# Up weights of the experts loaded in the last group of heads, down weights split in seven groups, five of eight rests by PE

## What is computed

```python
q  = ln(fp8_linear(ln_out, wq));  k = ln(fp8_linear(ln_out, wk));  v = fp8_linear(ln_out, wv)
core = softmax(q k^T) v                      # 16 heads in 8 groups
xout = softmax(ln(fp8_linear(ln_out, wqx)) ln(cond wkx)^T) (cond wvx)
x = layernorm(x + fp8(concat(core, xout)) wproj)

weights = softmax(softcap(x w_gate)) * top2_mask          # 8 experts, 2 of them per row
for e in range(8):
    out += (silu(x w1[e]) * (x w3[e])) w2[e] * weights[:, e]
x = layernorm(x + out)
```

## Time and profile before

| | us |
|---|---|
| median of 3 runs | 1407.73 (1407.22 to 1408.06) |
| the profiled execution | 1406.92 |
| its span, first to last instruction | 1405.2 |

### The profile page before, as it was taken

One profiled execution on the slowest core, in us unless ns is written; L12 is line 12 of the kernel. 1 busy time (PEld: TensorE's weight loads), 2 busy tenths in 40 slices (PEclk: granted clock), 3 DMA queues, 4 the chain that ended last, 5 costly groups with the idle time before them and its releaser, 6 DMA issues. The chain is left out here.

```text
span 1405.2 us, 28389 instructions
## 1 busy us (share of the span) xinstructions
PE 1317.8 (94%) x8483; PEld 1096.3 (78%) x8483; DVE 1044.0 (74%) x2583; ACT 940.9 (67%) x3183; POOL 917.5 (65%) x1109
## 2 busy tenths in 40 slices
PE   9999988896799999999999999999999978999992
PEld 4445666663599999999998998999898855899891
DVE  5899768897788888888887777777778847444443
ACT  3997457775588888888887777777777746323321
POOL 4996237774278787787887766766767844455542
PEclk9999999998999999999999999999999999999996
DMA  9421110000102002012020020020100248677764
GB/s 343 158 117 64 36 46 2 1 2 1 60 1 91 1 1 92 1 39 73 24 97 14 1 91 1 16 76 2 46 1 24 76 157 322 149 162 164 164 159 135
DMA packets 55160, 105.85 MB, mean 75 GB/s; under 512 B 5052, under 2 KB 33668, under 8 KB 52708
## 3 DMA queue, kind: packets, MB, share of 16 engines
q1 hardware_dynamic: 46100, 84.90, 17.7%
q0 software_dynamic: 7488, 10.23, 4.6%
q10 hardware_dynamic: 1424, 8.91, 1.6%
HBM read 75.58 MB, written 28.44 MB: 74 GB/s over the span
## 5 line engine op out<-in xcount | busy, mean ns | idle before, releaser
L1921 ACT ACTIVATE pr_<-ps,neg_ 128x128 f32<-128x128 f32 x512 | 181.1, 367 | 61.4 <-DVE neg_ L2091 61.4
L1938 ACT ACTIVATE y<-ps,invsm 128x128 bf16<-128x128 f32 x512 | 145.9, 368 | 62.3 <-PE ps L1826 62.0
L1999 POOL TENSOR_TENSOR rstd<-var,half 128x6 f32<-128x6 f32 x128 | 172.5, 1348 | 10.0
L2010 POOL TENSOR_TENSOR z<-t,m 128x512 fp32r<-128x512 bf16 x128 | 148.7, 1161 | 3.4 <-DVE t L2117 3.4
L1808 PEld LDWEIGHTS ps<-qkt 128*128 128x128 f32 x1024 | 134.0, 191 | 10.4 <-ACT qkt L1905 2.8
L1994 POOL TENSOR_TENSOR var<-stat,deps 128x6 f32<-128x6 f32 x128 | 26.1, 204 | 175.1 <-DVE stat L2071 175.0
L1837 PE MATMUL ps<-phi,z 128*128 128x256 f32 x512 | 138.1, 303 | 1.0 <-POOL z L2010 1.0
L1808 PE MATMUL ps<-qkt 128*128 128x128 f32 x1024 | 135.3, 275 | 2.5 <-ACT qkt L1913 2.3
L1826 PE MATMUL ps<-spare 128*128 128x256 f32 x512 | 131.9, 379 | 2.8 <-ACT spare L1929 2.8
L2003 POOL TENSOR_TENSOR pr_<-pr_,rec_ 128x512 f32<-128x512 f32 x128 | 132.7, 1037 | 1.8 <-DVE rec_ L2098 1.8
L1837 PE MATMUL ps<-plo,z 128*128 128x256 f32 x512 | 127.7, 280 | 0.0
(11 more groups left out here) (367 smaller groups left out, 4046.3 us busy)
## 6 DMA issues: line engine op xcount, KB each, us to landing
f_w_low<-w_low SPq DMA_DIRECT2D x39, 512.0 KB
centred<-raw_weights ACTq DMA_DIRECT2D x8, 1024.0 KB, 3.9
w_low<-w_dram SPq DMA_DIRECT2D x8, 1024.0 KB, 10.7
aw_st<-centred SPq DMA_DIRECT2D x7, 1024.0 KB, 6.3
raw_weights<-wself_dram SPq DMA_DIRECT2D x4, 1024.0 KB, 13.7
raw_weights<-wcross_dram SPq DMA_DIRECT2D x4, 1024.0 KB, 14.4
w_rest<-w_dram SPq DMA_DIRECT2D x8, 512.0 KB, 3.9
w_high<-w_top SPq DMA_DIRECT2D x8, 512.0 KB, 3.0
```

The costliest lines, as they stand in the source:

```text
L1921: ins = act.activation(pr[:, u.par, h, :], bS[:, h * S:(h + 1) * S], ACT.Exp, bias=neg[:, u.par, h:h + 1], accum_out=tot[:, u.par, h:h + 1])
L1938: ins = act.activation(y[:, u.par, h * S:(h + 1) * S], bO[:, h * S:(h + 1) * S], ACT.Copy, scale=invsm[:, head:head + 1])
L1999: pool.tensor_tensor(rstd[:, u.par, 0:6], v, half[:, :], ALU.pow).then_inc(s_rstd, 1)
L2010: pool.tensor_tensor(z[:, u.par, :], t[:, u.par, :], m[:, u.par, :], ALU.subtract).then_inc(s_z, 1)
```

## The change

- The tile of up weights (`w_low`, 64 KB per partition) is placed at the right end of memory, over tiles of the attention stage that are dead in its last group: slot 0 of `whi`, `wlo`, `phi`, `plo`, the codes of the values (now a tile of its own, `xval`), the raw weights, the raw context and both tiles of the down-weight split. The turned rows and the codes for the cross queries move to the left end.
- SP issues all eight loads of up weights at place 6 of the last group, after five waits (`load_up`).
- The split of the down weights is therefore done within the first seven groups: sixteen halves at places 3 and 13 of these and at place 8 of groups 1 and 4; SP stores a finished expert and loads the next one in the same step.
- The gate layer loads the high parts of the down weights; ACT rounds pieces 0 and 2 in it.
- PE makes the rests of five pieces instead of four (0, 2, 3, 5, 7), of which 2, 3 and 5 stand ahead of the map; only 7 stands behind it. VectorE is left with 1, 4 and 6. ACT's order is 3, 5, 1, 7, 4, 6, with the copies between (`HIGH_ORDER`).

```diff
-WARM_UNITS, WARM_PRODUCTS, WARM_AT_END, BY_PE = 4, (3, 4), 15, (0, 2, 3, 7)
+WARM_UNITS, WARM_PRODUCTS, WARM_AT_END, BY_PE = 4, (3, 4), 15, (0, 2, 3, 5, 7)
+HIGH_ORDER = (0, 2, 3, 5, 1, 7, 4, 6)
...
+        with ExitStack() as home:
+            up = sbuf(home, "w_low", [P, 2, E, 2 * I], F32R, side="right")
...
+        w2_units = sorted([B * w + b for w in range(2 * PAIRS - 1) for b in (3, 13)] + [B + 8, PAIRS * B + 8])
+
         def w2_half(u):
 
-            return slice(0, I) if u.b == 3 else slice(I, 2 * I) if u.b == 13 else None
+            if u.n not in w2_units:
+                return None
+            e, half = divmod(w2_units.index(u.n), 2)
+            return e, half, slice(half * I, (half + 1) * I)
...
+                def store_w2(u):
+                    if w2_half(u) is None:
                         return
...
+                    e, half, part = w2_half(u)
+                    if half:
+                        sp.wait_ge(s_w2_low, 2 * e + 2)
+                        for name, a in (("w2_high", w2_high), ("w2_low", w2_low)):
+                            sp.dma_start(io[name][e, :, :], a[:, :].bitcast(F32)).then_inc(w2_stored, 16)
+                        if e + 1 < E:
+                            load_w2(e + 1)
+
+                def load_up(u):
+                    if not u.last or u.b != UP_AT:
                         return
...
+                    sp.wait_ge(s_w, u.w * B)
+                    sp.wait_ge(weights.s_lo, weights.count(u.w, PIECES - 1))
+                    sp.wait_ge(weights.s_plo, weights.count(u.w, 1, 2))
+                    sp.wait_ge(s_clo, B)
+                    sp.wait_ge(w2_stored, 16 * 2 * E)
+                    for q in range(UP_PIECES):
+                        i, e = up_place(q)
+                        sp.dma_start(up[:, i, e, :].bitcast(F32).rearrange("p e (k n) -> p e k n", k=CB),
+                                     io[("w1", "w3")[i]][e].rearrange("e (k p) n -> p e k n", p=P)).then_inc(up_loaded[q], 16)
...
-                in_steps([(load_w2, 0), (load_weights, 0), (load_context, 0), (store_w2, 0), (store_rows, 7)])
+                in_steps([(first_w2, 0), (load_weights, 0), (load_context, 0), (store_w2, 0), (load_up, 0), (store_rows, 7)])
...
@@ gate_layer
-                experts.load_up(sp, io, range(0, UP_PIECES // 2))
                 for name in ("rows_x", "sums"):
                     sp.dma_start(io[name][(B - 1) * S:B * S, :], X[:, B - 1, :]).then_inc(experts.stored, 16)
+                experts.load_w2(sp, io)
...
                 experts.split_high(act, 0)
+                experts.split_high(act, 2)
...
@@ moe_layer, SP
-                experts.load_up(sp, io, range(UP_PIECES // 2, UP_PIECES))
-                experts.load_w2(sp, io)
...
@@ moe_layer, PE
                 subtract(2)
+                subtract(3)
+                subtract(5)
                 for c in range(2 * B // CHUNK):
...
-                subtract(3)
                 subtract(7)
...
@@ moe_layer, ACT
-                experts.split_high(act, 1)
                 keep(0)
-                experts.split_high(act, 2)
                 experts.split_high(act, 3)
                 keep(2)
-                for q in range(4, UP_PIECES):
+                experts.split_high(act, 5)
+                keep(3)
+                experts.split_high(act, 1)
+                keep(5)
+                for q in (7, 4, 6):
                     experts.split_high(act, q)
-                keep(3)
                 keep(7)
...
@@ moe_layer, VectorE
                 experts.split_low(dve, 4)
-                experts.split_low(dve, 5)
                 experts.split_low(dve, 6)
```

More of the change, by code:

```diff
@@ L185, in build @@
                     w2_stored = nc.alloc_semaphore(name="w2_stored")
-                    layer(quant_layer, columns_ctx, rows_ctx, row_stats, quant, rows_stored, w2_stored)
+                    up_loaded = [nc.alloc_semaphore(name=f"experts_up_loaded{q}") for q in range(UP_PIECES)]
+                    layer(quant_layer, xcross, up, up_loaded, row_stats, quant, rows_stored, w2_stored)
         args.pop("XT")
         if stop > 5:
-            experts = Experts(ctx, sbuf, nc, rows_stored, w2_stored)
+            experts = Experts(ctx, sbuf, nc, up, up_loaded, rows_stored, w2_stored)
             layer(gate_layer, experts)
@@ L1384, with __init__ @@
 class Weights:
-    def __init__(self, tag, quant, first, io, sem, sbuf, ctx):
+    def __init__(self, tag, quant, first, io, sem, sbuf, ctx, side="left"):
         self.quant, self.first, self.io = quant, first, io
-        self.st = sbuf(ctx, tag + "st", [P, PIECES, UW], F32)
-        self.rows = sbuf(ctx, tag + "rows", [P, 2, 2, C], F32)
+        self.st = sbuf(ctx, tag + "st", [P, PIECES, UW], F32, side=side)
+        self.rows = sbuf(ctx, tag + "rows", [P, 2, 2, C], F32, side=side)
         self.d_w, self.d_p, self.s_hi, self.s_lo, self.s_phi, self.s_plo = (
@@ L1611, in in_steps, with attention @@
                 stage(Pair(step - lag))
-def attention(xq, xcross, row_stats, quant, rows_stored, w2_stored, nc, io, sem, sbuf, X, XT, small, ident, ps, col, cols):
+def attention(xq, xval, xcross, up, up_loaded, row_stats, quant, rows_stored, w2_stored, nc, io, sem, sbuf, X, XT, small, ident, ps, col, cols):
     ctx = ExitStack()
@@ L1861, in _ @@
                 for _ in range(WARM_AT_END):
-                    pe.matmul(bQ[:, :], columns(CROSS, 0)[:, 0, :], whi[:, 1, 0, 0, :], start=True, stop=True)
+                    pe.matmul(bQ[:, :], columns(CROSS, 0)[:, 0, :], whi[1][:, 0, 0, :], start=True, stop=True)
             @block.scalar
@@ L1894, in prepare @@
                         weights.rows_high(act, u.w + 1, i)
-                    part = w2_half(u)
-                    if part is not None:
-                        act.wait_ge(d_w2, 16 * u.w + 16)
+                    if w2_half(u) is not None:
+                        e, half, part = w2_half(u)
+                        act.wait_ge(d_w2, 16 * e + 16)
                         act.activation(w2_high[:, part], w2_low[:, part].bitcast(F32), ACT.Copy).then_inc(s_w2_high, 1)
@@ L1983, in prepare @@
                         weights.rows_low(pool, u.w + 1, i)
-                    part = w2_half(u)
-                    if part is not None:
-                        pool.wait_ge(s_w2_high, 2 * u.w + 1 + (part.start > 0))
+                    if w2_half(u) is not None:
+                        e, half, part = w2_half(u)
+                        pool.wait_ge(s_w2_high, 2 * e + half + 1)
                         pool.tensor_tensor(w2_low[:, part], w2_low[:, part].bitcast(F32), w2_high[:, part].bitcast(F32),
@@ L2139, in _, with up_place, __init__ @@
                 dve.wait_ge(s_last_normed, 1)
+UP_AT = 6
+def up_place(q):
+    e, i = divmod(q, 2)
+    return i, slice(e * PIECE, (e + 1) * PIECE)
 class Experts:
-    def __init__(self, ctx, sbuf, nc, stored, w2_stored):
+    def __init__(self, ctx, sbuf, nc, up, up_loaded, stored, w2_stored):
         self.gate = sbuf(ctx, "moe_gate", [P, CB, ROWS], F32)
-        self.low = sbuf(ctx, "w_low", [P, 2, E, 2 * I], F32R)
         self.high = sbuf(ctx, "w_high", [P, 2, E, 2 * I], F32R)
         self.w2 = sbuf(ctx, "w2", [P, E, 2 * I], F32R)
-        self.up_loaded = [nc.alloc_semaphore(name=f"experts_up_loaded{q}") for q in range(UP_PIECES)]
+        sbuf(ctx, "w_low_home", [P, 2, E, 2 * I], F32R, side="right")
+        self.low, self.up_loaded = up, up_loaded
         self.w2_loaded, self.s_hi, self.s_lo = (
@@ L2349, in chunks @@
         def chunks(q):
-            i, e = experts.place(q)
+            i, e = up_place(q)
             first = BY_PE.index(q) * PIECE * CB
@@ L2385, in subtract @@
                 def subtract(q):
-                    pe.wait_ge(experts.s_hi, q + 1)
+                    experts.made_high(pe, q)
                     for at, (i, e, c) in chunks(q):
```

106 lines of the change are left out of this document (50 added, 56 removed).

## The result

| | before, us | after, us |
|---|---|---|
| median of 18 runs each | 1413.43 (1407.22 to 1416.61) | 1415.88 (1414.60 to 1419.66) |
| the profiled execution | 1406.92 | 1415.52 |
| its span | 1405.2 | 1413.8 |

The account below looks back on a forecast made before the run. The kernel's end was taken to stand where the expert loop's chain of 39 scatter-adds starts; a later map less time saved behind it moved the first up product by +3.1 us, so 1407.73 + 3.1 = 1410.8 us, range 1406.5 to 1413.2.

Parts of the forecast that it names:

- The gathers, taken as hidden: Behind the token list: the second gather of x lands at 1190.5, 2.7 us after issue, hidden under VectorE's splits.
- the terms of VectorE (1.49, 4.40, 0.80): From list to first up product: 1.49 us to the next splits, 4.40 for two splits, 0.80 from rest of x.
- Rival 1: Behind the list: the second gather trails VectorE's last split, first up product at 1193.2, +4.7 us, 1412.4 us; chance 0.18.
- saves 2.2 us behind the list: Piece 5 taken off VectorE saves 2.2 us behind the list and costs 4.4 us ahead of it.
- Part 1: Last group of heads: eight 1 MB loads of up weights, about 1051 to 1073 us, are covered and cost 0.
- rival 4: Attention stage: the 8 MB of loads slow it by 0.5 us or more, giving 1411.3 to 1413 us; chance 0.07.
- its own sign: Train of adds: the prediction is wrong if the train's own step, 4.8 us, changes; only its start should move.
- Part 2: Attention stage: the sixteen down-weight halves, done within seven groups, cost 0 in sum.
- Part 3: Gate layer: with weights in place, ACT's rounding ends sooner and the next layer starts 0.83 us earlier.
- Part 4: Ahead of the map: twelve chunks instead of four, map at 1177.45, 7.7 us new wait; first up product +3.1 us.
- Rival 2: Ahead of the map: PE's clock does not fall, map at 1175.7, first product +1.4 us, 1409.1 us; chance 0.33.
- Rival 3: Ahead of the map: chunks run faster without transfers, at 0.65 us each -3.9 us, 1403.8 us; chance 0.10, other gains included.

Follow-up runs that it names:

- lower group: The kernel before, unchanged, in its faster executions: five of its 18 runs, from 1407.2 to 1408.1 us.
- upper group: The kernel before, unchanged, in its slower executions: thirteen of its 18 runs, from 1413.1 to 1416.6 us; the profiled one took 1413.27 us.

## Why the prediction was right and wrong

The forecast was +3.1 us on 1407.73, that is 1410.8 us and +0.22%, in a range of 1406.5 to 1413.2. The time of the changed kernel, 1415.88 us, lies outside. Set against what the forecast stood on, an execution of the lower group, the change cost 8.2 us in the medians and 8.6 in the profiles. The ratio, +0.28%, is near the forecast by luck, as the paragraph on the level shows. Counted in steps of the two profiles:

| step | forecast | measured |
|---|---|---|
| start of the gate layer | 0 | +1.31 |
| to piece 0 | -0.83 | -0.83 |
| to the map | +7.73 | +5.95 |
| to the list | 0 | -0.08 |
| to the first up product | -3.76 | -0.92 |
| to the first add | 0 | +1.67 |
| first to last add | 0 | +1.3 |
| sum | +3.1 | +8.4 |

**The gathers, taken as hidden.** This is the step that failed. The sum had the second gather in under the splits, at the 2.7 us of the quickest row. It took 6.54 from its issue to PE's use, and from the list to the first up product it took 9.53 us, where the sum had 6.69: 2.8 us too few. With the rests of the down weights held back it was 6.59, so the terms of VectorE (1.49, 4.40, 0.80) were right and the gather was the missing one. That run's median, 1412.21, lies inside the range: it was this wait and the cold first tile behind it, 4.5 us together, that took the time out of the range.

Rival 1 named the gather, but for the wrong reason and from a misread row: it had it trail VectorE's splits by 2.1 us, 8.2 behind the list. In the row of PE's weight load the wait is put down to the gather; PE's own row of the same products, shown above, names VectorE's rest of x, as it does in every profile of the kernel before. The gather was beside the same three loads there, and at the 6.54 us measured after it would have been in at 1187.4 (an estimate), ahead of 1188.31. So the 10.45 us behind the list covered it, and the change shortened what covered it. For the same reason the prediction's "saves 2.2 us behind the list" is too little: its own sum gains 3.76 there, 1.56 of it because PE's piece 3 no longer stands behind the map.

The Trainium skill (SBUF — State Buffer, "SBUF: two separate sides") has a transfer issued by GpSimd seem blocked while VectorE holds the shared port pair. It says so for VectorE's two-port modes; for an instruction with two SBUF operands, like the splits, it names only a conflict with GpSimd instructions that read SBUF. The run with the rests held back shows that the 3 us were not such a block: the gather came that much sooner under the same splits. What the splits do go with is a longer issue on POOL, 1.7 to 1.9 us, against 0.95 behind them. In another place the trace agrees with that section, which has one engine wait for a whole instruction of the other: the router's instructions of 0.17 us took 1.2 beside POOL's of 1.27.

**Behind the first product.** The prediction moved the loop as a block. But PE's 3.48 us of waiting for the gather put the clock to 0.57 at 1194 to 1198, and the first tile took 1.67 us more. Without that wait it took 10.3 again.

**Part 1, the loads at no cost.** Right in the attention stage: first to last residual 745.9 us after, 746.5 before, the loads issued at 1052.18 and the next row store at 1073.36. The step of the residuals went from 6.12 to 6.27 us at 1058, but in the kernel before it did so too, at 1057. So rival 4 did not come. Wrong for what the loads need: the new place of the tiles costs 1.3 to 1.6 us in the loop. The prediction priced the transfers and the waits of this part, and the place of an operand not at all. By its own sign, that the train's step must not change, it was wrong here: 4.85 us a step instead of 4.82.

**Part 2, seven groups, no cost.** Right, by the same stretch.

**Part 3, the gate layer, -0.83.** Right, to the hundredth by luck: in the other profiles of the kernel before the same stretch was up to 0.6 us shorter.

**Part 4, the map.** The mechanism was right, the size 1.8 us off: the map stands 5.1 us later counted from the gate layer, where the forecast had 6.9, because the clock fell already at piece 0 (0.57 at 1156 to 1160) and the twelve chunks ran every 1.09 us (1163.89 to 1175.89). Rival 2 has the same map, 1175.7, exact when 1.3 us of later start is added (1176.98), but not for its reason: it had the clock hold because the gap at the layer's start was shorter, and the clock fell right behind that gap. Rival 3, faster chunks without transfers, is refuted: a chunk took 1.09 us with the DMA share at 0.00, as it had at 1.02.

**The level of before.** The sum was set on 1407.73 us, the median of three runs, and on one profile, all of the lower group. On 18 runs the kernel before has 1413.43, 5.7 us more. This did not make the forecast time wrong, since the changed kernel has no such groups; it hid part of the loss, 5.7 us in the medians and 4.6 in the means, and so brought the ratio near the forecast. The profile showed the sign of it: a gap of 0.82 us ahead of the map that was short only because piece 2 had run slowly, 6.13 us for 4.36. The prediction used that fall as a cost that stays, and asked in rival 2 what its absence would save. It never followed the shorter piece 2 into the gap behind it, which then is 0.82 + 1.77 = 2.6 us (2.48 in the execution of the upper group), and cools the map for 5 us. The change makes one group of the two: twelve chunks run into the map without a gap, so every execution pays the late map, where the kernel before pays the slow map in some.

So the four steps from the gate layer's start to the first up product, which the forecast summed to +3.1, were in fact -0.83 + 5.95 - 0.08 - 0.92 = +4.1 (a map 1.8 us less late and a gather that shows), and two it did not have, +1.7 and +1.3, make +7.1. The rest of the 8.2 against the lower group is the later start of the gate layer, which the spread of the profiles doesn't let us put down to the change. Against the mix of both groups the change is +4.0.

What stays open: why the clock falls in one execution at piece 0, in the next at piece 2 and in a third ahead of the map, with gaps of nearly the same length ahead of the counting products (2.19 us in the profile of before, 2.18 in the execution of the upper group); what sets the share of the two groups on an occasion; and how the loads hold up the gather.

## What to carry to other kernels

Before a profile serves as the level for a sum, look for a short gap that is short only because something ahead of it ran slowly: the next execution may have the fast piece and the long gap, and the price of a gap is that of the work behind it. Don't fill an early gap and leave the one right ahead of the expensive products: closing only the first moved the fall of the clock to the worst place (+0.4%), closing both took the upper group away. And when a gather on the critical path is issued beside bulk loads that nobody needs yet, hold the loads back by one wait: it gave 3 us here.

## What the hardware showed beyond that

- The clock did not come back while the map ran: at 1173 to 1183 us of the execution of the upper group PE was busy for all 10 us and the granted clock stayed at 0.50. It rose only in the subtractions behind the map, and was at 1.00 from 1186.
- A gap ahead of the map was followed by the fall in each of the four profiles that had a long one (2.48, 2.49, 2.59 and 3.23 us), and in none of the four with one of 0.3 to 1.04 us.
- The place of operands in memory changes the pitch of fp32r products by 1.5% (0.2355 to 0.2390 us) with nothing else different.
- A gather issued beside three loads of 512 KB reached PE after 6.5 us, one issued ahead of them after at most 3.6.
